# Rounded sums one step later, values by two multiply-adds, a shorter shift, and 128-row matmuls in the first stage

## The reference

```python
q = _fq_sym(q, axis=-1); k = _fq_sym(k, axis=-1)       # s = max|x|/127, round(x/s)*s
v = _fq_sym(v, axis=2)                                 # one scale over all keys
attn = jax.nn.softmax(jnp.einsum('bhqd,bhkd->bhqk', q, k), axis=-1)
attn = _fq_unsigned(attn, axis=-1)                     # s = max/255, round(attn/s)*s
out = jnp.einsum('bhqk,bhkd->bhqd', attn, v)
```

## Time and profile before

| | |
|---|---|
| median of 3 runs | 4641.71 us (4641.0 to 4643.88) |
| the profiled execution's own time | 4639.28 us |
| its span, from first to last instruction | 4636.2 us |
| first stage | 0 to about 733 us |
| heads 0 to 14 | about 742 to 3970 us |
| last head | about 3971 to 4200 us |
| the rest (last sums, projection, second layer, experts) | to 4636 us |
| busy: PE, DVE, ACT, POOL | 96%, 87%, 76%, 80% |
| mean granted clock of TensorE | 0.982 of 2.4 GHz |

### The profile page before, as it was taken

One profiled execution on the slowest core, in us unless ns is written; L12 is line 12 of the kernel. 1 busy time (PEld: TensorE's weight loads), 2 busy tenths in 40 slices (PEclk: granted clock), 3 DMA queues, 4 the chain that ended last, 5 costly groups with the idle time before them and its releaser, 6 DMA issues. The chain is left out here.

```text
span 4636.2 us, 150451 instructions
## 1 busy us (share of the span) xinstructions
PE 4459.4 (96%) x54175; PEld 1971.5 (43%) x54175; DVE 4037.1 (87%) x7370; ACT 3531.4 (76%) x3643; POOL 3692.6 (80%) x4025
## 2 busy tenths in 40 slices
PE   7999998999999999999999999999999999888999
PEld 5666663333333333333333333333333333224665
DVE  6788888999999999999999999999999999774333
ACT  3555557889889898989898988989898989873121
POOL 5777776899999999999999999999999999772000
PEclk9999997999999999999999999999999999998999
DMA  3555542111111111111111111111111111442010
GB/s 101 150 164 161 171 148 66 35 35 33 35 33 34 35 34 35 33 34 34 33 35 35 32 36 33 34 35 35 34 33 35 34 33 32 144 155 91 0 38 8
DMA packets 222771, 268.77 MB, mean 58 GB/s; under 512 B 34366, under 2 KB 202809, under 8 KB 221289
## 3 DMA queue, kind: packets, MB, share of 16 engines
q1 hardware_dynamic: 167529, 203.57, 15.8%
q10 hardware_dynamic: 54528, 55.60, 3.8%
HBM read 174.57 MB, written 82.97 MB: 56 GB/s over the span
## 5 line engine op out<-in xcount | busy, mean ns | idle before, releaser
L1546 ACT ACTIVATE e_home<-ps_scores,sk 125x896 f32<-125x896 f32 x3072 | 3076.2, 1008 | 388.7 <-ACTq L1545 204.3
L1579 DVE TENSOR_REDUCE unit_max<-ps_maxima 128x1 f32<-128x428 f32 (+2 forms) x5760 | 3115.2, 607 | 54.4 <-DVEq L1576 40.9
L1764 POOL TENSOR_SCALAR r<-e_home 125x896 f32<-125x896 f32 x2976 | 2769.6, 954 | 287.1 <-ACT e_home L1546 114.7
L1349 PE MATMUL ps_maxima<-e_home,unit 125*17 125x224 f32 x24576 | 1705.7, 354 | 12.2 <-PEq L1333 7.6
L1321 PE MATMUL ps_maxima<-k_home,q 48*128 48x428 bf16 (+2 forms) x5760 | 1614.8, 350 | 15.8 <-issue 1.8
L1293 PE MATMUL ps_scores<-q,k_home 54*128 54x448 bf16 x5760 | 1592.7, 356 | 4.8 <-PEq L1468 2.9
L1341 PE MATMUL ps_maxima<-r,vt 125*16 125x224 f16 x12288 | 854.5, 267 | 60.8 <-PEq L1335 30.7
L1293 PEld LDWEIGHTS ps_scores<-q,k_home 54*128 54x128 bf16 x5760 | 329.6, 95 | 1064.0 <-issue 1034.7
L1341 PEld LDWEIGHTS ps_maxima<-r,vt 125*16 125x16 f16 x12288 | 300.3, 86 | 783.0 <-issue 780.7
L1349 PEld LDWEIGHTS ps_maxima<-e_home,unit 125*17 125x17 f32 x24576 | 620.0, 95 | 19.2 <-issue 17.0
L1321 PEld LDWEIGHTS ps_maxima<-k_home,q 48*128 48x128 bf16 x5760 | 524.2, 93 | 233.3 <-issue 63.7
(11 more groups left out here) (270 smaller groups left out, 2723.6 us busy)
## 6 DMA issues: line engine op xcount, KB each, us to landing
k_rows<-krows ACTq DMA_DIRECT2D x48, 1000.0 KB, 7.0
k_home<-k_rows SPq DMA_DIRECT2D x408, 93.8 KB
k_home<-k_rows SPq DMA_DIRECT2D x120, 281.2 KB
e_home<-in_ctxT SPq DMA_DIRECT2D x48, 500.0 KB, 4.2
vr<-v_raw SPq DMA_DIRECT2D x128, 187.5 KB
cb<-in_ctxT SPq DMA_DIRECT2D x16, 1500.0 KB, 6.1
v_raw<-e_home SPq DMA_DIRECT2D x12, 1000.0 KB
v_raw<-vb SPq DMA_DIRECT2D x12, 1000.0 KB
```

What stands on the lines that cost most here:

```text
L1349: made = pe.matmul(psav[c:c + WIDE, lo:hi], unit[:, :], e[(i + s) % SLOTS][0:KT, g, lo:hi], start=head_first and part == 0, stop=False, sk ...
L1546: act.activation(e[i % SLOTS][0:KT, :, :], score_banks(i)[0:KT, :, :], ACT.Exp, scale=sk[u][:, i:i + 1]).then_inc(e_wrote[h % 2], 1)
L1579: top = dve.tensor_reduce(maxima[y][:, b, slot:slot + 1], ps[:, 0:hi - lo], axis=AX.X, op=ALU.max)
L1764: pool.tensor_scalar(r[i % SLOTS][:, :, :], e[i % SLOTS][0:KT, :, :], 1.0, WHOLE_WORD, ALU.mult, ALU.add)\
```

## The change

- `LAG` is 6, and the parity of the two parts is turned: step 6 makes part 0 of the pair (0, 1), step 7 part 1. ACT's copy of the sums moves to after step 5. After the last head one more part is issued behind the loop.
- The exponent's shift no longer holds ln 255. The exponentials are at most 1, and the rounding multiplies by 255 instead of 1.0; the constant in `unit` that takes the rounding offset out grows by the same factor. The minus sign is multiplied into the scales `sq` once, in the first stage.
- The shift's parts are made in five operations: product, first part written to three columns at once, remainder, second part to two columns, third part. The order of the six columns changes, and with it `T_ROWS`, which says which rows of `t_rows` each part of the scales fills. DVE's version at the end of the first stage changes alike.
- The values are rounded over all 384 elements at once: a multiply-add in place after step 7 (`raised_values`), and a multiply-add into f16 after step 10 (`whole_values`), joined by semaphores in place of POOL's waits for its own results.
- In the first stage `bias`, `ones` and `q0` have 128 rows, zero beyond the old ones in `bias` and `q0`; the pieces multiply all 128 rows of the block of `rows`, without a tile position. DVE clears `bias`, POOL clears `q0`.

```diff
+    HIGH, MID, LOW = slice(0, SROWS, 2), slice(1, SROWS - 1, 2), SROWS - 1
+    T_ROWS = ((0, 1, 5), (2, 3), (4,))
...
     def scaled_values(h, half):
...
-        pool_done(pool.tensor_tensor(part, part,
-                                     v_inv[:, bass.ds(h * HDIM, HDIM)].rearrange("p (o d) -> p o d", o=1)
-                                     .to_broadcast([KT, VTILES, HDIM]), ALU.mult))
-
-    def whole_values(x, half):
-        tiles = slice(half * VTILES, (half + 1) * VTILES)
-        pool_done(pool.tensor_scalar(x[:, tiles, :], vr[:, tiles, :], ROUND, ROUND, ALU.add, ALU.subtract))
+        pool.tensor_tensor(part, part,
+                           v_inv[:, bass.ds(h * HDIM, HDIM)].rearrange("p (o d) -> p o d", o=1)
+                           .to_broadcast([KT, VTILES, HDIM]), ALU.mult).then_inc(v_scaled, 1)
+
+    def raised_values():
+
+        pool.wait_ge(v_scaled, 2).then_inc(v_scaled, -2)
+        pool.tensor_scalar(vr[:, :, :], vr[:, :, :], 1.0, ROUND, ALU.mult, ALU.add).then_inc(v_raised, 1)
+
+    def whole_values(x):
+        pool.wait_ge(v_raised, 1).then_inc(v_raised, -1)
+        pool_done(pool.tensor_scalar(x[:, :, :], vr[:, :, :], 1.0, -ROUND, ALU.mult, ALU.add))
         pool.sem_inc(vt_ready, 1)
...
-        bias = sbuf(st, "k_bias", [PARTS, 2 * DIM], bf16)
-        ones = sbuf(st, "k_ones", [PARTS, KT], bf16)
+        bias = sbuf(st, "k_bias", [P, 2 * DIM], bf16)
+        ones = sbuf(st, "k_ones", [P, KT], bf16)
...
-        q0 = sbuf(st, "q0", [HROWS, TOK], bf16)
+        q0 = sbuf(st, "q0", [P, TOK], bf16)
...
-                    pe.matmul(first_bank(n, b)[:, 0:GK], q0[:, b * QB:(b + 1) * QB],
-                              rows[n % 2][0:HROWS, DIM // P, :], start=True, stop=True, tile_position=(0, 0))\
-                      .then_inc(s_full, 1)
+                    pe.matmul(first_bank(n, b)[:, 0:GK], q0[:, b * QB:(b + 1) * QB], rows[n % 2][:, DIM // P, :],
+                              start=True, stop=True).then_inc(s_full, 1)
...
+            dve.wait_ge(sq_landed, 16).then_inc(sq_landed, -16)
+            dve_done(dve.tensor_scalar(sq[:, :, :], sq[:, :, :], -1.0, None, ALU.mult))
...
-    LAG = 5
+    LAG = 6
...
-    SCALED, WHOLE, CHAINED = (1, 4), (SLOTS - 1, SLOTS + 2), 13
+    SCALED, RAISED, WHOLE, CHAINED = (1, 4), 7, 10, 13
...
-                    at = i - LAG - (1 - i % 2)
+                    at = i - LAG - i % 2
...
-                pool_done(pool.tensor_scalar(shift[:, :], shift[:, :], -1.0, LOG255, ALU.mult, ALU.add))
-                for part in range(2):
-                    pool_done(pool.tensor_copy(shift_parts[:, :, part], shift[:, :]))
-                    rest = shift[:, :] if part == 0 else shift_parts[:, :, 2]
-                    pool_done(pool.tensor_tensor(rest, shift[:, :], shift_parts[:, :, part], ALU.subtract))
-                pool_done(pool.tensor_copy(shift_parts[:, :, 3:5], shift_parts[:, :, 0:2]))
-                pool.tensor_copy(shift_parts[:, :, 5], shift_parts[:, :, 0]).then_inc(shift_ready, 1)
+                pool_done(pool.tensor_copy(shift_parts[:, :, HIGH], shift_copies(3)))
+                pool_done(pool.tensor_tensor(shift[:, :], shift[:, :], shift_parts[:, :, 0], ALU.subtract))
+                pool_done(pool.tensor_copy(shift_parts[:, :, MID], shift_copies(2)))
+                pool.tensor_tensor(shift_parts[:, :, LOW], shift[:, :], shift_parts[:, :, 1], ALU.subtract)\
+                    .then_inc(shift_ready, 1)
...
-                pool.tensor_scalar(r[i % SLOTS][:, :, :], e[i % SLOTS][0:KT, :, :], 1.0, WHOLE_WORD, ALU.mult, ALU.add)\
+                pool.tensor_scalar(r[i % SLOTS][:, :, :], e[i % SLOTS][0:KT, :, :], LEVELS, WHOLE_WORD, ALU.mult, ALU.add)\
                     .then_inc(r_ready, 1)
...
-            pool_done(pool.memset(unit[:, HDIM:], HALF_UNIT))
+            pool_done(pool.memset(unit[:, HDIM:], LEVELS * HALF_UNIT))
```

More of the change, by code:

```diff
@@ L55 @@
 WHOLE_WORD = 8388608.0
+LEVELS = 255.0
 HALF_UNIT = 2.0 ** -24
@@ L744, in dve_program @@
             dve_done(dve.tensor_tensor(bias_part[2], bias_rest, bias_part[1], ALU.subtract))
-            dve_done(dve.tensor_scalar(bias[:, :], bias_part[0], ident[0:PARTS, 0:1], None, ALU.mult))
-            dve_done(dve.scalar_tensor_tensor(bias[:, :], bias_part[1], ident[0:PARTS, 1:2], bias[:, :],
-                                              ALU.mult, ALU.add))
+            dve_done(dve.memset(bias[:, :], 0.0))
+            own = bias[0:PARTS, :]
+            dve_done(dve.tensor_scalar(own, bias_part[0], ident[0:PARTS, 0:1], None, ALU.mult))
+            dve_done(dve.scalar_tensor_tensor(own, bias_part[1], ident[0:PARTS, 1:2], own, ALU.mult, ALU.add))
             dve_done(dve.memset(ones[:, :], 1.0))
-            dve.scalar_tensor_tensor(bias[:, :], bias_part[2], ident[0:PARTS, 2:3], bias[:, :],
-                                     ALU.mult, ALU.add).then_inc(bias_ready, 1)
+            dve.scalar_tensor_tensor(own, bias_part[2], ident[0:PARTS, 2:3], own, ALU.mult, ALU.add)\
+               .then_inc(bias_ready, 1)
             dve_done(dve.memset(v_tops[:, 0, :], 0.0))
@@ L852, in pool_program @@
             pool.wait_ge(bv_landed, 16).then_inc(bv_landed, -16)
+            pool_done(pool.memset(q0[:, :], 0.0))
+            pool.sem_inc(q0_cleared, 1)
             for n in range(NGEN):
@@ L905, in pool_program @@
                 scaled_values(0, half)
-                whole_values(vt0, half)
+            raised_values()
+            whole_values(vt0)
         def act_program():
@@ L950, in copy_scales @@
                 act.sem_inc(turn_free, 1)
-                for row in ((0, 1, 2), (3, 4), (5,))[r]:
+                for row in T_ROWS[r]:
                     act.dma_start(t_rows[row, batch].rearrange("(q b) k -> q b k", b=TB), t_rows_sb[:, r, :, :])\
@@ L1457, in step_sums @@
                     elif at >= 0:
-                        sums(at, u, 1 - i % 2, shared=not first)
+                        sums(at, u, i % 2, shared=not first)
                     elif not head_start or finished is not None:
-                        sums(at + CT, 1 - u, 1 - i % 2, head_end=head_start and i == LAG - 1,
+                        sums(at + CT, 1 - u, i % 2, head_end=head_start and i == LAG - 1,
                              shared=not first and not head_start)
@@ L1516, in pe_program @@
             last.then_inc(x_sum_ready, 1)
+            sums(CT - 6, 1, 0, shared=True)
             last_exponentials(CT - 2)
@@ L1612, in rounded @@
                 dve.wait_ge(e_wrote[(HEADS - 1) % 2], j * CT + i + 1)
-                dve.tensor_scalar(r[i % SLOTS][:, :, :], e[i % SLOTS][0:KT, :, :], 1.0, WHOLE_WORD, ALU.mult, ALU.add)\
+                dve.tensor_scalar(r[i % SLOTS][:, :, :], e[i % SLOTS][0:KT, :, :], LEVELS, WHOLE_WORD, ALU.mult, ALU.add)\
                    .then_inc(r_odd, 1)
@@ L1775, in chunk @@
                         scaled_values(h, SCALED.index(i))
-                    if h is not None and i in WHOLE:
-                        if i == WHOLE[0]:
-                            pool.wait_ge(v_free[1 - u], 1).then_inc(v_free[1 - u], -1)
-                        whole_values(vt[1 - u], WHOLE.index(i))
+                    if h is not None and i == RAISED:
+                        raised_values()
+                    if h is not None and i == WHOLE:
+                        pool.wait_ge(v_free[1 - u], 1).then_inc(v_free[1 - u], -1)
+                        whole_values(vt[1 - u])
             pool.sem_inc(v_free[1], 1)
```

24 lines of the change are left out of this document (12 added, 12 removed).

## The result

The changed kernel takes 4676.9 us (median of 4 runs, 4671.8 to 4681.2), the kernel before 4642.8 in the same comparison: a ratio of 1.0071, 95% interval 1.0053 to 1.0088. It is 34 us slower; 4537 was forecast, 105 us faster.

The account below looks back on a forecast made before the run. PE was taken to set the pace, with DVE close behind; 44 (first stage) + 42 (heads) + 20 (last head) - 1 = 105 us off the 4641.7 us median gave 4537 us, range from 5 us below 4487 up to 4595.

Parts of the forecast that it names:

- The rounding itself, with 255 in place of 1.0, is the same instruction.: POOL's and DVE's rounding of the weights: the new multiplier was given no price.
- Rival 4: Values on POOL: both multiply-adds at the cast's rate, 3.8 us, choke POOL; heads lose 60 us, 4658 us; chance 0.03.
- The values: POOL, each chunk: two multiply-adds of 0.52 us each, 1.04 instead of 1.72, and three self-waits of some 0.2 us gone.
- rival 3: Values on POOL: the second multiply-add, writing f16, runs at the old rate, 1.5 us; 4549 us; chance 0.08.
- The heads: Heads before the last: step, shift and values end PE's pauses and small waits; 42 us gained, bounds 20 and 51.
- the windows round the shift: Four steps round each head's shift: 108.4 us where 64.2 would do; 35 of the 44 counted, DVE being next late.
- Pause, low clock and small waits: Heads: PE's 1.97 us pause at the shift, the low clock after it and 7 us of small waits would end.
- rival 2: Heads: DVE's maxima take over as the bound, so heads give 12 instead of 42; 4567 us; chance 0.12.
- The first stage: Full-height bias and pieces save PE 1.9 us a generation, 1.0 taken for each of 44: 44 us, bounds 0 and 70.
- rival 1: First stage: matmul height costs nothing, the extra time being weight loads, so 128 rows gain nothing; 4581 us; chance 0.14.
- DVE lets 1.4 of them through at most: First stage: of PE's 1.9 us saved a generation, DVE, 1.4 us behind PE, would allow at most 1.4.
- Last head: Last head: one step's delay removes half or all of each wait for a rounding; 20 us gained, bounds 8 and 35.

Follow-up runs that it names:

- a_scale1: The changed kernel with 1.0 instead of 255.0 in the two rounding lines, so weights round to 0 or 1; 4566.9 us, ratio 0.9831.
- best_six: The changed kernel with roundings at 1.0 and ln 255 added by a sixth small POOL operation in the shift; 4566.7 us, ratio 0.9831.
- best_bias: The changed kernel with roundings at 1.0 and ln 255 as the bias operand of ACT's exponential; 4575.4 us, ratio 0.9851.
- b_probe: The kernel before without ln 255, POOL's rounding given another multiplier every three steps, one read from SBUF; only distances read, no time given.

## Why the prediction was wrong

**The step that failed.** "The rounding itself, with 255 in place of 1.0, is the same instruction." It is, by its duration (938 to 942 ns), but not by its distance to its neighbours: 1.02 us instead of 0.90. 24 of them a chunk are 24 x 0.115 = 2.8 us, 22 us a head. The text counted the rounding at 0.92 and put no price on the constant, though everything in the heads hangs on it. What POOL had to spare a head is in a_scale1's group (760 to 3900 us, 14.8 heads):

```profile
L1779 POOL TENSOR_SCALAR r<-e_home 125x896 f32<-125x896 f32 x2834 | 2630.2, 941 | 253.5 <-ACT e_home L1563 69.0 <-POOLq L104 39.9 <-POOLq L318 20.0
```

Without the 39.9 us until its own results, which stay, that is 14 us a head. So some 8 of the 22 should come to the surface, 7.3 do, and with the last head it is 110 us, the distance from 4567 to 4677. Nothing in the trace of before showed another constant; what it did show is how little room POOL had. Rival 4 worked that out: 1.04 us for the multiply-adds were forecast, 3.7 were the turning point, so POOL's room was 2.7 us a chunk. Its mechanism, POOL choked and PE waiting for rounded values, is the one that came, with 2.8 us from another line. That its time, 4658 us, lies near the measured one is partly luck, since it takes the first stage at 44 us; with the measured 20 its sum gives 4682.

**The values.** Two multiply-adds of 0.51 us (the groups after); 0.52 were taken. The second writes f16 and costs the same, so rival 3 falls.

**The heads.** With a cheap constant, 14 x 3.1 = 43 us, and the windows round the shift give 108.4 - 70.8 = 37.6; forecast 42 and 35. Pause, low clock and small waits went as described, and DVE didn't take their place, so rival 2 falls. But that 35 came so close is luck: the text took 9 of the 44 off because DVE would be late next. In best_six PE is busy through all 70.8 us of the windows, and DVE for 65.6. So PE itself needs 6.6 us more there than the 64.2 of the text. What the text didn't see is that the later sums or the values alone would have brought most of the gain (36 and 39 of 43 us), the shift half of it (22).

**The first stage.** 19 us for 44. The passages between heights were sized rightly, even low (from a bias matmul to the next matmul 0.25 us became 0.11, where 0.18 was forecast), so rival 1 falls: of the two pages of the Trainium skill that the prediction set against each other, "TensorEngine Tiling (Array Packing)", section "Key Properties", agrees with the trace, with some 0.1 us for a passage. PE's busy time in 500 to 660 us falls by 20 of 157 us, 1.7 us a generation, but a generation gets only 19.4 / 44 = 0.44 us shorter. The step "DVE lets 1.4 of them through at most" mistook idle time for room; which wait takes its place is open, as said above.

**Last head and the rest.** 20 us were forecast; with a cheap constant it is 7 to 12 (214.0, 211.5, 217.1 us in three such kernels). The stages' terms, 20 + 43 + 10 = 73, make the 72 us between the spans of best_six (4564.0) and before; the forecast's 105 was 24 too high in the first stage and 10 in the last head, and lacked the 110 of the constant.

## What to carry to other kernels

Where an engine has little room (here POOL, idle some 16 of 215 us a head), price each instruction by the distance between starts in a back-to-back run, not by its duration, and treat any edit to it, even of a constant, as a new instruction until a run of it is seen. Edits that each remove the same pause don't add up: measure one, then ask what is left. Idle time of the next engine in line isn't yet room that a faster neighbour can use: here 17.6 us of it in 12 generations let 5 through.

## What the runs showed of the hardware

- GpSimd's multiply-add of 125x896 f32 has two paces, 0.90 and 1.02 us from start to start, at one recorded duration of 0.94 us, by the multiplier that stands in the instruction: 255.0 and 256.0 differ. The gap of 0.08 us, in place of an overlap of 0.04, stands on both sides of the dear one and also before and after other operations, such as the scaling of the values (1602.21, 0.08 us after the end of the row before). What is dear in it isn't known.
- A bias operand read per partition costs ScalarE 91 ns a call of 896 elements (1099 for 1008, best_bias), a multiplier read per partition costs GpSimd 74 ns (1012 for 938, b_probe).
- A passage between 3 or 48 and 125 or 128 rows costs TensorE 0.10 to 0.14 us, by the distances that fell in the first stage (0.31 to 0.21, 0.53 to 0.43, 0.25 to 0.11).
